# GNN, mixer and expert layers on one core: two of the sixteen weight-sum chunks move from TensorE to VectorE

## What is computed

```python
def rgcn_gate_layer(x, row, col, edge_type, basis, att, gate_w, root, bias):
    w = jnp.einsum('rb,bio->rio', att, basis)     # 2 relations, 30 bases of 512x512
    x_j = x[col]
    msgs = []
    for r in range(2):
        gate = jax.nn.sigmoid(x_j @ gate_w[r, :, 0])
        msgs.append(gate[:, None] * x_j @ w[r])
    msg = jnp.where((edge_type == 0)[:, None], msgs[0], msgs[1])
    return jax.ops.segment_sum(msg, row, num_segments=x.shape[0]) + x @ root + bias
```

## Time and profile before

| | us |
|---|---|
| median of 3 runs | 500.25 |
| the profiled execution | 503.05 |
| its span | 501.3 |
| TensorE busy | 453.6 (90%) |
| VectorE busy | 216.6 (43%) |
| ScalarE busy | 166.6 (33%) |
| GpSimd busy | 183.1 (37%) |

### The profile page before, as it was taken

How to read it: one execution, slowest core, us unless ns; L and a number is a source line. 1 busy time by engine, 2 the same in 40 slices (tenths; PEclk the granted TensorE clock), 3 DMA queues, 4 the chain that set the end, 5 groups by cost and what they waited for, 6 DMA issues and landing times.

```text
span 501.3 us, 7256 instructions
## 1 busy us (share of the span) xinstructions
PE 453.6 (90%) x2592; PEld 319.6 (64%) x2592; DVE 216.6 (43%) x447; ACT 166.6 (33%) x365; POOL 183.1 (37%) x205
## 2 busy tenths in 40 slices
PE   2799899979999999798999999999999999999980
PEld 2354346758765664375657787777777778875760
DVE  5779981231352535644222002342002658752563
ACT  2699774222220011731115004225006460133310
POOL 3112100065230441189060890621504644950522
PEclk9999999998999999899999999999999999999995
DMA  5999999857999978965910716040002183999646
GB/s 124 389 425 420 424 424 377 319 234 277 371 397 408 406 249 311 418 255 180 298 80 1 224 68 251 1 107 3 5 1 63 43 319 105 282 344 356 204 150 198
DMA packets 38787, 119.26 MB, mean 238 GB/s; under 512 B 7050, under 2 KB 7111, under 8 KB 30302
## 3 DMA queue, kind: packets, MB, share of 16 engines
q1 hardware_dynamic: 33276, 111.17, 59.5%
q0 software_dynamic: 3360, 3.86, 3.4%
q10 hardware_dynamic: 2114, 3.74, 2.0%
HBM read 103.92 MB, written 14.82 MB: 237 GB/s over the span
## 4 chain that ended last, share of the span: by engine, by line
PE 81%; issue 6%; DVE 4%; POOL 3%; DMA 2%; ACT 2%; DVEq 1%; POOLq 0%
PE ps L1647 15%; PE ps L1649 13%; PE ps L1648 13%; PE ps L1671 11%; PE ps L2006 9%; PE ps L1732 5%; PE ps L2141 2%; PE ps L2131 2%; PE ps L1851 2%; PE ps L2153 1%; DMA got<-y_dram,slot_u 1%; PE ps L1655 1%; DVE oh_n L954 1%; PE ps L2118 1%; DMA y_dram<-ybuf 1%
## 5 line engine op out<-in xcount | busy, mean ns | idle before, releaser
L1671 PE MATMUL ps<-ring,sel_att 128*32 128x512 f32 x512 | 66.8, 609 | 5.2 <-PE ps L1671 2.0
L1647 PE MATMUL ps<-piece_hi,ht_hi 128*125 128x512 f32 x140 | 56.1, 401 | 0.8 <-PE ps L1649 0.6
L1105 DVE SCALAR_TENSOR_TENSOR u_lo<-ps,gates,u_hi 125x512 fp32r<-125x512 f32 x20 | 15.0, 751 | 94.1 <-ACT u_hi L1528 94.1
L1648 PE MATMUL ps<-piece_lo,ht_hi 128*125 128x512 f32 x140 | 55.1, 394 | 0.0
L1649 PE MATMUL ps<-piece_hi,ht_lo 128*125 128x512 f32 x140 | 55.1, 394 | 0.0
L746 POOL CAST piece_hi<-piece_raw 128x512 fp32r<-128x512 f32 x28 | 20.0, 713 | 95.9 <-issue 56.6
L747 POOL TENSOR_TENSOR piece_lo<-piece_raw,piece_hi 128x512 fp32r<-128x512 f32 x28 | 37.1, 1326 | 14.1 <-issue 11.9
L2006 PE MATMUL ps<-u_hi,cf 125*125 125x512 f32 x100 | 39.9, 399 | 1.3 <-PE ps L1649 1.3
L2006 PE MATMUL ps<-u_lo,cf 125*125 125x512 f32 x100 | 39.4, 394 | 0.0
L954 DVE TENSOR_SCALAR oh_n<-iota_n,keys 125x626 f16<-125x626 f16 x100 | 32.2, 392 | 9.0 <-PE ps L1732 7.0
L1732 PE MATMUL ps<-oh_n,oh_m 125*128 125x313 f16 x200 | 31.5, 314 | 4.6 <-DVE oh_m L955 4.6
(11 more groups left out here) (332 smaller groups left out, 929.4 us busy)
## 6 DMA issues: line engine op xcount, KB each, us to landing
ring<-in_L_gnn_basis_dram SPq DMA_DIRECT2D x64, 1024.0 KB, 8.1
w_home<-in_L_ffn_W_sp_dram SPq DMA_DIRECT2D x27, 256.0 KB, 5.7
rel_dram<-stag SPq DMA_DIRECT2D x16, 256.0 KB, 7.9
w_raw<-rel_dram SPq DMA_DIRECT2D x8, 512.0 KB, 6.6
w_fq<-in_L_ffn_W_fq_dram SPq DMA_DIRECT2D x2, 2048.0 KB, 11.1
y_dram<-ybuf ACTq DMA_DIRECT2D x13, 256.0 KB, 5.2
piece_raw<-in_L_mix_Wkqv_dram SPq DMA_DIRECT2D x3, 1024.0 KB, 9.5
x_dram<-stag SPq DMA_DIRECT2D x1, 3072.0 KB
```

Source lines behind the costliest of these rows:

```text
L1105: dve.scalar_tensor_tensor(out=u_lo[l][:, t, :], in0=ps[0:TP, u_bank(i), :], scalar=gates[:, t, r:r + 1], in1=u_hi[l][:, t, :].bitcast(F32 ...
L1647: pe.matmul(target, a_hi, b_hi, start=first, stop=False, skip_group_check=skip)
L1648: pe.matmul(target, a_hi, b_lo, start=False, stop=False, skip_group_check=skip)
L1671: last = pe.matmul(ps[32 * c:32 * c + 32, rel_bank(ch), :], sel_att[:, ch // CHUNKS, g].rearrange("p r q -> p (r q)"), ring[slot][:, c * D ...
```

## The change

Chunks 6 and 7 of layer 2 are no longer summed by TensorE. There are 56 parts in place of 64. VectorE takes these two chunks: its 128 partitions hold 64 of each, 512 elements wide, and for each of 30 bases and 2 relations it does one multiply-add on them (`sums`), 60 instructions. SyncE loads them in 60 pieces of 128 KB in place of 8 of 1 MB (`load_for_vector`), in two turns through four ring slots. The sums lie in `v_sum`, and the factors in `att_all`, broadcast by one more DMA. `store_sum(r)` stores the sum of relation r, and `read_second(r)` reads that relation's weights back.

The split of rel2_0 leaves GpSimd: ScalarE makes the high half (`high_of_second`) and VectorE the low half (`low_of_second`). GpSimd's addition of x to y moves behind the split of root2.

```diff
-PARTS = 2 * CHUNKS * NG
+V_CHUNKS = 2
+P_CHUNKS = 2 * CHUNKS - V_CHUNKS
+PARTS = P_CHUNKS * NG
...
+            load_for_vector(0, 0)
+            load_for_vector(0, 1)
+            store_chunk(P_CHUNKS - 2)
+            load_for_vector(0, 2)
+            store_chunk(P_CHUNKS - 1)
+            load_for_vector(0, 3)
+            load_piece("root2")
             sp.wait_ge(hT_t, NT)
             for a, b in ROWS:
                 sp.dma_start(x_again[a:b, :, :], x.rearrange("(t p) n -> p t n", p=TP)[a:b]).then_inc(x_in, 16)
-            read_relations(1)
+            for s in range(4):
+                load_for_vector(1, s)
+            for r in range(REL):
+                store_sum(r)
+                read_second(r)
...
-            pool.wait_ge(x_in, 64)
-            for t in range(NT):
-                pool.wait_ge(xm_ready, t + 1)
-                pool.tensor_tensor(y[:, t, :], y[:, t, :], x_again[:, t, :], ALU.add).then_inc(xm_plus_x, 1)
-            split("rel2_0")
             for s in rel_out:
-                pool.wait_ge(s, 16 * CHUNKS)
+                pool.wait_ge(s, 16 * (P_CHUNKS // 2 + V_CHUNKS))
             pool.memset(stag[:, 0, :], 0.0).then_inc(consts_ready, 1)
+            pool.wait_ge(split_done, PIECE["rel2_0"] + 1)
             split("root2")
...
+            SUMS = [(b, r) for b in range(16) for r in range(REL)] + [(b, r) for r in range(REL) for b in range(16, BASES)]
+                    dve.wait_ge(basis_in[s], 16 * (V_AT[s] + V_CHUNKS * len([a for a in V_OF[s] if a // 16 <= turn_])))
...
+                        step = dve.scalar_tensor_tensor(out=target, in0=source, scalar=factor, in1=target, op0=ALU.mult, op1=ALU.add)
...
             for c in range(KT):
...
                 dve.tensor_tensor(act_lo[:, c, :], act_tmp[:, c % 2, :], act_hi[:, c, :].bitcast(F32), ALU.subtract).then_inc(act_ready, 1)
+                sums((0, 2, 1, 2)[c])
...
             for t in range(NT):
+                sums(2)
                 dve.wait_ge(w2_mm, t + 1)
...
             def messages(l):
+                if l == 0:
+                    sums(1)
                 dve.wait_ge(gate_mm, l + 1)
                 dve.tensor_copy(in_halves(gate_row[:]), ps[0:2 * REL, 0:2, 0:HALF]).then_inc(gate_row_ready, 1)
+                if l == 0:
+                    sums(6)
...
+                        if l == 0:
+                            sums(2)
+                    if a == 0:
+                        sums(46 - summed[0])
+                        sums(5)
+                        low_of_second()
...
-                    relation_parts((1, 1, 1, 0)[c])
+                    relation_parts((1, 1, 0, 0)[c])
...
                 if t + 1 < NT:
                     turn_xn(t + 1)
-                relation_parts(1)
...
                 if l == 0:
-                    relation_parts(PARTS - part[0])
+                    assert part[0] == PARTS
                     pe.wait_ge(xm_ready, 3)
```

More of the change, by code:

```diff
@@ L200, in gnn_mix_ffn @@
         kq_lo = place("kq_lo", [128, KT, NPAD], F32R, r_u + KB628)
+        v_sum = [place(f"v_sum{i}", [128, D], F32, a) for i, a in enumerate((r_bias + 2 * D * 4, r_bias + 3 * D * 4, r_stag))]
+        att_all = place("att_all", [128, REL * BASES], F32, r_bias + 5 * D * 4 + 1024)
         y = place("y", [TP, NT, D], F32, r_u)
@@ L318, in gnn_mix_ffn @@
         w_in, router_in = sem("w_in"), sem("router_in")
[L319 to L322 removed]
+        w2_in, W2_SEEN = [w_in, edges_in, att_in, smalls_in, rel_back[2]], [16, 48, 32, 176, 48]
+        w1_fq_in, W1_FQ_SEEN, w1_moved, w1_moved_dve = rel_back[0], 48, sem("w1_moved"), sem("w1_moved_dve")
+        V_AT = [WIDE // 8 + (PARTS - WIDE) // 4] * 4
+        V_OF = [[b for b in range(BASES) if b // 4 % 4 == s] for s in range(4)]
+        RING_SEEN = [V_AT[s] + V_CHUNKS * len(V_OF[s]) for s in range(4)] + [3] * 4
+        y_out, Y_SEEN = (basis_in[0:3], basis_in[3:8]), [[16 * RING_SEEN[i] for i in r] for r in (range(3), range(3, 8))]
+        w2_fq_in, W2_FQ_SEEN = rel_back[1], 48
         k_hi_done = sem("k_hi_done")
@@ L555, in _ @@
                 load_part(i)
-            piece_after = {11: "k", 24: "q", 27: "v", 30: "Wo", 34: "W1", 40: "W2", 50: "root1", 62: "root2"}
+            piece_after = {11: "k", 24: "q", 27: "v", 30: "Wo", 34: "W1", 40: "W2", 50: "root1"}
             chunk = 0
@@ L559, in _ @@
                 load_part(i)
-                while chunk < 2 * CHUNKS and i >= min(NG * chunk + (12 if NG * chunk + 12 <= WIDE else 9), PARTS - 1):
+                while chunk < P_CHUNKS - 2 and i >= min(NG * chunk + (12 if NG * chunk + 12 <= WIDE else 9), PARTS - 1):
                     store_chunk(chunk)
@@ L795, in _ @@
             own_step(pool.memset(b1_raw[:], 0.0))
+            pool.wait_ge(x_in, 64)
+            for t in range(NT):
+                pool.wait_ge(xm_ready, t + 1)
+                pool.tensor_tensor(y[:, t, :], y[:, t, :], x_again[:, t, :], ALU.add).then_inc(xm_plus_x, 1)
             split("rel2_1")
@@ L1094, in _, with low_of_second @@
             many = dve.value_load(many_i[0:1, 0:1], min_val=0, max_val=1)
+            def low_of_second():
+                s, p_hi, p_lo = piece("rel2_0")
+                dve.wait_ge(split_done, s)
+                for t in range(KT):
+                    dve.wait_ge(k_hi_done, KT + t + 1)
+                    last = dve.tensor_tensor(p_lo[:, t, :], w_raw[:, t, 0, :], p_hi[:, t, :].bitcast(F32), ALU.subtract)
+                last.then_inc(split_done, 1)
             def messages(l):
+                if l == 0:
+                    sums(1)
                 dve.wait_ge(gate_mm, l + 1)
                 dve.tensor_copy(in_halves(gate_row[:]), ps[0:2 * REL, 0:2, 0:HALF]).then_inc(gate_row_ready, 1)
+                if l == 0:
+                    sums(6)
                 dve.wait_ge(gates_ready, l + 1)
@@ L1510, in unit_round, with high_of_second @@
                     act.activation(hi, raw, ACT.Copy).then_inc(unit_hi, 1)
+            def high_of_second():
+                s, p_hi, _ = piece("rel2_0")
+                act.wait_ge(piece_used, s - 1)
+                for t in range(KT):
+                    act.wait_ge(rel_back[t], 16 * 2)
+                    act.activation(p_hi[:, t, :], w_raw[:, t, 0, :], ACT.Copy).then_inc(k_hi_done, 1)
             def messages(l):
```

85 lines of the change are left out of this document (63 added, 22 removed).

## The result

| | before | changed |
|---|---|---|
| median | 501.37 us (498.81 to 504.72, 20 runs) | 497.43 us (494.86 to 500.89, 20 runs) |
| ratio of the times | 1 | 0.9931, 95% interval 0.9906 to 0.9956 |
| profiled execution, its span | 503.05, 501.3 us | 496.16, 494.4 us |
| mean granted clock of TensorE in it | 0.981 | 0.984 |

The change makes the kernel 0.7% faster: 3.5 us by the ratio, 3.9 us by the medians. Forecast were 3.55 us and 496.7 us.

The account below looks back on a forecast made before the run. TensorE, busy 90% of the span, was taken to bound the kernel. 1.3 + 2.8 + 1.45 - 2.0 = 3.55 us off a 500.25 us median gave 496.7 us (chance 0.42); the range ran from B, less 1.2 us, to 501.5 us.

Parts of the forecast that it names:

- W1, +1.3: First product: without its part W2 starts earlier; three VectorE sums ahead of the last `act_hi` cost 0.1; gain 1.3 us.
- W2's four parts, +4.0 gross: Second product: four weight-sum parts behind its first tiles go, each standing for 0.99 us, 4.0 us together.
- W2's stalls, -1.2: Second product: sums at 1.4 us beside GpSimd make `ht_lo` late; TensorE stalls 0.5 and 0.7 us.
- second stall of 0.7 us: Second product, next tile: VectorE needs 4.0 us against TensorE's 3.44 us, so TensorE stalls 0.7 us.
- Rival A: Each sum waits out a whole GpSimd instruction and costs 1.65 us; gain 1.65 us, 498.6 us; chance 0.24.
- The last three parts, +1.45: Ahead of the gates: of 3.1 us, 1.45 is won; the rest becomes a wait for VectorE's last `y` and `ht_lo`.
- Six sums ahead of `u_lo`, -2.0: Behind the gates: six sums take 7.2 us beside GpSimd's split of root1; TensorE stalls 2.0 us at the third message tile.
- Rel2_0's road, 0: Sum, store, read-back, then split by ScalarE and VectorE near 298.5 us: hidden at no cost, some 2 us of cover.
- The rest at nothing: Split of root2, later addition of x, zeroing of `x_dram`, evacuations and 60 small loads cost nothing; x1 needed near 388 us.
- B: Sums cost 0.7 to 0.9 us throughout, no stall: gain 6.85 us, 493.4 us; chance 0.14.
- C: Slow store and reads make rel2_0 late; TensorE stalls 7.3 us at relation 1's third tile: 504.0 us; chance 0.11.
- D: The removed parts only filled waits, so TensorE waits where it worked and nothing is won: 500.2 us; chance 0.09.

Follow-up runs that it names:

- experiment 1: Changed kernel with VectorE's sums moved out from between the GELU splits of W1's loop: 495.47 us, ratio 0.9866 to the kernel before.
- experiment 3: Changed kernel with 57 of the 60 sums left out, the three plain multiplications, loads, waits and stores kept: 496.07 us, ratio 0.9896 to the kernel before.
- Experiment 2: Changed kernel with 24 useless TensorE transposes filling the idle time ahead of W2: 495.22 us, ratio 0.9881 to the kernel before.
- Experiment 7: Changed kernel with the six sums ahead of the first `u_lo` cut into three and three by a VectorE wait: 498.43 us, ratio 0.9938.
- experiment 8: Changed kernel with GpSimd's addition of x put back where the kernel before has it: 501.89 us, ratio 1.0013 to the kernel before.
- experiments 5 and 6: Changed kernel, no sums in W1's loop, two or all three parts between W1's start and W2 put behind the first turn: 493.90 and 492.49 us.

## Why the prediction was right, and where not

**The total** (3.55 us forecast, 3.5 by stages, 3.9 by medians) and "faster" were right. The likeliest case was sums at two prices and most of the gain kept. The sum came out by luck: against the forecast W1 lost 2.0 us and the clock 2.4, while W2's parts gave 1.0 more, its stalls 1.2, the last three parts 0.2 and the six sums 2.0, which together is nothing. Its terms:

- *W1, +1.3.* Wrong, and the step that failed most plainly: "VectorE has three sums ahead of the last `act_hi`, and finishes them about when GELU delivers ... I take 0.1 us for that." GELU did come 1.6 us sooner. But VectorE was 2.0 us late for it, since the sums (1.5 and 1.75 us each) and the third group's `act_hi` and `act_lo` (1.57 and 1.78) follow each other without a gap. The error was in weighing only the sums against GELU, and not the whole chain of VectorE from the second group on. In it the third `act_hi` takes 1.57 us, for 0.51 before and 0.54 in experiment 1, all beside GpSimd's same additions; why it is short in one case and long in the other was not tested. Instead of +1.3 came -0.7; experiment 1 gets 1.26 of it back, and experiment 3 shows that the sum behind the third group is what costs it.
- *The clock, not in the sum.* 3.66 us of idle time ahead of W2 cost another 2.4 us, because the first tile ran at 1.2 GHz. Experiment 2 shows it.
- *W2's four parts, +4.0 gross.* They gave more, 5.0: turns of before are 4.45 us apart (236.16, 240.61), of now 3.24, and four such steps plus their small idle times make 4.45 + 4.45 + 4.69 + 4.53 for 3.28 + 3.24 + 3.24 + 3.40. A part's row of 0.99 us does not hold the step over to it and back.
- *W2's stalls, -1.2.* Not there, because the slow first tile gave VectorE its time. Where the clock is full (experiment 2) they are 0.5 us, with the first four sums at 5.5 us for 5.6 forecast. That price was right. The forecast's second stall of 0.7 us does not follow from its own 4.0 against 3.44 us, which leaves 0.56; a step of 3.24 us from turn to turn would give 0.76. Rival A's 1.2 us has the same slip.
- *The last three parts, +1.45.* Right: 3.12 us from block to gates before, and 1.46 us of waiting for `ht_lo` now, +1.66.
- *Six sums ahead of `u_lo`, -2.0.* Wrong: nothing. The step "of six sums four cost 1.4 us and two 0.7" took the price of sums that alternate with GpSimd. In a train that starts as GpSimd's cast does, they take 0.68 each and GpSimd waits. Experiment 7 brings a part of the price back, 0.97 us a sum, and a stall of 0.5 us. The forecast's sum slips here too: four at 1.4 and two at 0.7 are 7.0 us, not 7.2, and by the same count rival A's stall is 2.8 us and not 2.4.
- *Rel2_0's road, 0.* Right, and "the cover is short: some 2 us" too: experiment 8 is late by 5.2 us and stalls TensorE by 2.9, so 2.3 were covered. Against the gates the sum was whole 2.4 us sooner than forecast (35.0 for 37.4), and the road behind it took 10.8 us for 9.5, together 1.1 us sooner. Store and reads were close to the short values (store issued 285.43, first `piece_hi` 291.02, last 294.80: 9.4 us for 8.7).
- *The rest at nothing.* Right in the time, but the text priced the later addition of x only as a cost, "x1 needs it near 388". That it had to leave the stretch in which VectorE sums, or rel2_0 would be late, was not seen; it holds up the whole gain.

**The rivals.** *A* (a whole GpSimd instruction waited, 1.65 us) has rows for and against: 1.75 us for the sum at 225.93, 1.37 at 230.20, 0.68 at 253.50. As one price it is wrong, and so is the forecast's 1.4. The Trainium skill (SBUF — State Buffer, section "SBUF: two separate sides") has the lock held by whoever starts first, for its instruction. The train at 253.50 is more than that, since a cast of 0.61 us stood through six sums. *B* (0.7 to 0.9 us throughout, +6.85) is wrong for W1 and W2 and right behind the gates. *C*'s mechanism exists: experiment 8 is it, with VectorE's sums as the cause and not the transfers, and it decides about 2.3 us from where the change stands. *D* is wrong: the parts did not fill waits, except that in W1 one can fill one, which experiments 5 and 6 use.

**What would show it.** Gates near 251.6: they came at 250.30, but in a profile that is 3.4 us ahead at W1; on the clock of before that is 253.7, two us late, and beyond the 253 that the text had set as a sign of being wrong. The 2 us ahead of the third tile and the short stalls by `ht_lo` were absent. The marks told what the total hid.

## What to carry to other kernels

Ahead of a point where TensorE waits, lay end to end everything that the feeding engine does from the last gap on, each at its price beside the others, not just the instructions added; and put TensorE's own spare work where it would stand idle, since in these kernels idle times of 2.3 to 4.0 us were paid for again by the clock behind them (1.5 to 2.4 us). When a total agrees, still compare it stage by stage with the forecast: here five terms were off by 1.0 to 2.4 us and cancelled. And when a change moves several things at once, undo each alone: the least regarded move (GpSimd's addition of x, worth 4 us) carried the gain, and the one that looked clever (the split by two engines) carried nothing.
